# A bound of two on the gathers that GpSimd has unfinished in three graph passes

## The chip, the cores and the metric

The kernel runs on one core of a Trainium2 chip. The metric is the device time of one execution in microseconds (us). The kernel before takes 12057.81 us, the median of three runs (12056.52 to 12058.14).

## The reference

There are 12500 nodes with 48 features and 212500 directed edges, sorted by destination. Four residual layers follow each other, and each starts from relu(layernorm(x)):

```
L0: x = x + segment_sum(h[src] * edge_weight, dst)
L1: gate(edge) * h[dst] * cutoff(edge), summed by src, divided by a sum of multiplicities,
    added to h, layernorm, gamma, beta; x = x + that
L2: a = exp(e - segment_max) / segment_sum(exp); x = x + elu(segment_sum(h[src] * a, dst))
L3: y1 = spmm(h); y2 = spmm(y1); x = x + (h + y1 + y2) / 3
    with spmm(h) = segment_sum(h[src] * edge_weight, dst)
```

Three of these need the same work: gather one row per edge from a table in HBM, multiply it by a scalar of the edge, and sum by destination. These are the weighted sum of L2 and the two spmm of L3. They are the three passes that the change touches.

## The kernel before

Edges are padded to 1664 columns of 128 edges (one edge on each partition). Four columns make a group (G = 4), eight groups make a turn (GB = 8), and there are 416 groups in 52 turns. Nodes stand in blocks of 128. A group's destinations fall into one or more blocks; each pair of a group and a block is a window, and a pass has 512 of them.

The program runs five passes over the edges, one after the other, with short layernorm stages between them. `first_pass` does L0 (1668 gathers, line 504). The second pass does L1 and adds its result into HBM with 1664 scatters (line 1097). `light_pass` (line 720) runs three times, for L2, L3a and L3b, with 1664 gathers each (line 736).

In `light_pass` each engine runs its own loop:

- ScalarE converts the four index columns of a group into the `idx` tile (line 743), and later multiplies each of the group's four gathered tiles in `ring` by the edges' weights (line 756), when the gathers have landed (line 753).
- GpSimd waits for a group's indices (line 733) and issues four indirect DMAs (line 736). Each gathers 128 rows of the table into one slot of `ring`. It waits for nothing else, so its sequencer may hand over gathers as far ahead as indices are staged. `idx` and `ring` have 32 slots (8 groups), and ScalarE stages six groups ahead (LEAD).
- VectorE builds a one-hot matrix of destinations for a window (`hot`, line 789), adds the sum of the window before to `acc` (line 778), and after a group's last window raises `s_done` (line 797). ScalarE stages the next group's indices only after that (line 749).
- TensorE multiplies the one-hot by the weighted rows into PSUM, four fp32 matmuls a window that the profile shows as eight (line 816).

Windows are counted in registers, so VectorE's sequencer runs a dozen register instructions for each (lines 774 to 796). The second pass issues its scatters differently: before each one GpSimd waits on one of K = 4 semaphores until the scatter four places earlier has landed (line 1095) and raises `s_seen` (line 1096). Semaphores are waited on by value and never reset; `order` is 0, 1, 2 for the three light passes.

Of the kernel before, what the change touches and what calls it, by code (L numbers as in the profile page):

```python
# [19 lines left out]
U = G * GB  # L20
NG = -(-E // (P * U)) * GB
T = NG * G
TURNS = NG // GB
# [3 lines left out]
AHEAD = 3  # L27
DEPTH = GB
LEAD = DEPTH - 2
TI = T + LEAD * G  # L30
PARTS = 3
C0 = C + GE
# [17 lines left out]
def gnn_kernel(nc, x, dst_cols, src_cols, dst_rows, src_rows, w_cols, logit_cols, logit_rows,  # L50
# [10 lines left out]
    with ExitStack() as ctx:  # L61
        def sb(name, shape, dt=f32):
            return ctx.enter_context(nc.sbuf_tensor(name, shape, dt))

        def sem(name):
            return ctx.enter_context(nc.semaphore(name))
# [21 lines left out]
        iota = sb("iota", [P, NBW * P], u16)  # L88
        dstf = sb("dstf", [P, TI])
        w = sb("w", [P, TI])  # L90
        cw = sb("cw", [P, T])
        lg = sb("lg", [P, TI])
        adapt = sb("adapt", [P, G + T])
        srow = sb("srow", [P, TI])
        ranges = sb("ranges", [1, NG * 2], i32)
# [12 lines left out]
        idx = sb("idx", [P, DEPTH * G], i32)  # L108
# [165 lines left out]
        with nc.Block() as block:  # L274
# [43 lines left out]
            def _(dve):  # L318
# [3 lines left out]
                for columns in (srow, dstf, w, lg):  # L322
                    nv.memset(columns[:, T:TI], 0.0)
                nv.memset(hid[:, :, :], 1.0)
# [137 lines left out]
        s_seen = sem("s_seen")  # L462
        s_landed_rows = [sem(f"s_landed_rows{j}") for j in range(DEPTH)]
        s_spread = sem("s_spread")
        s_picked = sem("s_picked")
        s_kept = sem("s_kept")
        wn_dve = nc.vector.alloc_register("dve_window")
        wn_act = nc.scalar.alloc_register("act_window")
        wn_pe = nc.tensor.alloc_register("pe_window")
# [250 lines left out]
        def light_pass(order, name, src_table, cols, weights, total, before=None):  # L720
# [7 lines left out]
            with nc.Block() as block:  # L728
                @block.gpsimd
                def _(pool):  # L730
                    with pool.Fori(0, TURNS) as i:
                        for j in range(GB):
                            pool.wait_ge(s_idx, i * GB + (j + 1))
                            pool.sem_inc(s_seen, 1)
                            for u in range(j * G, (j + 1) * G):
                                pool.indirect_dma_start(  # L736
                                    out=ring[:, u, 0:cols], out_offset=None, in_=src_table,
                                    in_offset=bass.IndirectOffsetOnAxis(ap=idx[:, u:u + 1], axis=0)).then_inc(s_landed_rows[j], 16)

                @block.scalar  # L740
                def _(act):
                    def stage(slot, column):
                        nc.scalar.copy(idx[:, slot * G:(slot + 1) * G], srow[:, ds(column, G)]).then_inc(s_idx, 1)  # L743

                    for j in range(LEAD):
                        stage(j, j * G)
                    with act.Fori(0, TURNS) as i:
                        for j in range(GB):
                            act.wait_ge(s_done, i * GB + (j + 1))
                            act.sem_inc(s_seen, 1)  # L750
                            stage((j + LEAD) % DEPTH, i * U + (j + LEAD) * G)

# [543 lines left out]
```

## Time and profile before

| | us |
|---|---|
| median of three runs | 12057.81 |
| span of the profiled execution | 14556.0 |
| GpSimd busy in it | 9189.0 |
| TensorE matmul busy | 6194.2 |
| VectorE busy | 4412.4 |
| ScalarE busy | 3916.7 |

The profiled execution is 2498 us longer than the median of the runs that nobody profiled. The profile gives no time for it beside its span. Its durations are those of one execution with the profiler on.
### The profile page before, as it was taken

Reading aid. Unit: us, or ns where it says so; the run is one execution under the profiler, and the core shown is the slowest. Engines: PE = TensorE matmul, PEld = TensorE weight load, DVE = VectorE, ACT = ScalarE, POOL = GpSimd, SP = SyncE. Lnnn points to the kernel's source line nnn. Section 1 sums busy time; section 2 is a strip of 40 time slices with the busy share of each in tenths; the row PEclk is TensorE's granted clock in tenths of the full one; section 3 lists DMA queues with packets and bytes.
Section 4 is the critical chain, followed back from the end, with each engine's and each line's share of the span. In section 5 each row is a group of like instructions: output and inputs, shape, how many; then the busy total and the mean of one; then the engine's idle time right before and its main releaser. Section 6 shows DMA issues by size and latency. Waiting matters only on the chain. (4 is left out here: it accounts for less than half of the span.)

```text
span 14556.0 us, 229228 instructions
## 1 busy us (share of the span) xinstructions
PE 6194.2 (43%) x41742; PEld 4831.3 (33%) x41743; DVE 4412.4 (30%) x18474; ACT 3916.7 (27%) x13496; POOL 9189.0 (63%) x8348
## 2 busy tenths in 40 slices
PE   4444444444555555552333333333333333333333
PEld 2222222223444444442333333233333333333333
DVE  4444444445444444443111111211111111111111
ACT  3444444443333333321111111111121111111111
POOL 5555555556888888884666666566666656666665
DMA  4333333334455554541111111111111111111111
GB/s 116 100 102 102 99 97 96 96 94 63 61 62 61 61 62 61 62 59 42 16 16 16 16 16 16 20 16 16 16 16 16 16 21 16 16 16 16 16 16 21
DMA packets 805020, 671.18 MB, mean 46 GB/s; under 512 B 417876, under 2 KB 663828, under 8 KB 802727
## 3 DMA queue, kind: packets, MB, share of 16 engines
q0 software_dynamic: 452736, 234.14, 14.8%
q1 hardware_dynamic: 349659, 430.53, 11.2%
q10 hardware_dynamic: 2588, 6.12, 0.1%
q14 instruction: 26, 0.21, 0.0%
q8 instruction: 11, 0.18, 0.0%
HBM read 562.94 MB, written 107.13 MB: 46 GB/s over the span
## 5 line engine op out<-in xcount | busy, mean ns | idle before, releaser
L736 POOL DMA_INDIRECT table<-table,idx x4992 | 4838.7, 969 | 3149.9 <-ACT idx L743 1638.0
L816 PE MATMUL psum_acc<-table 128*128 128x48 f32 (+1 forms) x12288 | 2946.7, 417 | 5074.1 <-DVE acc L778 2363.5
L816 PEld LDWEIGHTS psum_acc<-table 128*128 128x128 f32 x12288 | 2733.0, 328 | 5287.7 <-issue 5244.2
L1097 POOL DMA_INDIRECT sums<-rows,idx x1664 | 2619.5, 1574 | 577.6 <-issue 430.9
L504 POOL DMA_INDIRECT rows<-table,idx x1668 | 1670.2, 1001 | 1581.9 <-ACT idx L556 1059.2
L789 DVE TENSOR_TENSOR table<-iota,dstf 128x512 f32 x1536 | 1064.6, 693 | 3059.2 <-issue 2074.7
L743 ACT CAST idx<-srow 128x4 int32 (+1 forms) x1266 | 243.2, 193 | 6322.7 <-DVEq L797 4262.1
L778 DVE TENSOR_TENSOR acc<-acc,psum_acc x1539 | 311.3, 202 | 3420.0 <-remote 2352.8
L704 PE MATMUL psum_acc<-parts,onehot 128*128 128x48 bf16 x6144 | 338.8, 215 | 1600.5 <-DVE onehot L647 1433.7
L1013 PE MATMUL psum_exp<-table,onet 128*128 x6144 | 432.3, 219 | 1376.2 <-DVE onet L932 1166.2
L756 ACT ACTIVATE table<-table,w 128x48 f32<-128x48 f32 x3328 | 840.6, 323 | 26.2 <-DMA table<-table,idx 12.4
L1013 PEld LDWEIGHTS psum_exp<-table,onet 128*128 128x128 bf16 x6144 | 341.8, 116 | 1510.4 <-issue 1487.5
L704 PEld LDWEIGHTS psum_acc<-parts,onehot 128*128 128x128 bf16 x6144 | 271.8, 117 | 1686.8 <-DVE onehot L647 1500.9
L986 PE MATMUL psum_mlp<-w2s,hid 49*128 49x48 f32 x3336 | 808.3, 414 | 50.8 <-DMA hid<-hid_dram 50.7
L986 PEld LDWEIGHTS psum_mlp<-w2s,hid 49*128 49x128 f32 x3336 | 741.2, 324 | 124.5 <-issue 124.5
L597 ACT ACTIVATE scratch<-drow,far 128x512 f32<-128x512 uint16 x512 | 369.3, 721 | 598.8 <-DVE segmax L666 293.2
L1064 ACT ACTIVATE gate<-psum_mlp,adapt,cw 128x48 f32<-128x48 f32 x1664 | 514.1, 390 | 48.8 <-issue 26.2
L1043 ACT CAST parts<-rest 128x196 bf16<-128x196 f32 x416 | 149.9, 360 | 1281.1 <-DVE rest L913 903.8
L964 DVE TENSOR_TENSOR idx<-srow,dmp 128x4 int32<-128x4 f32 x416 | 67.9, 163 | 1321.3 <-POOLq L1099 1243.8
L691 PE MATMUL psum_mlp<-srcrow,w1s 40*48 40x512 f32 x416 | 396.9, 1056 | 153.3 <-issue 152.2
L573 ACT ACTIVATE prod<-rows,w 128x48 f32<-128x48 f32 x1668 | 426.0, 324 | 54.0 <-issue 39.9
L756 ACT ACTIVATE table<-table,lg 128x49 f32<-128x49 f32 x1664 | 422.0, 325 | 14.2 <-DMA table<-table,idx 9.1
(183 smaller groups left out, 7162.2 us busy)
## 6 DMA issues: line engine op xcount, KB each, us to landing
drow<-rows_dram SPq DMA_DIRECT2D x832, 128.0 KB
lrow<-in_logit_rows SPq DMA_DIRECT2D x416, 256.0 KB
table<-table,idx POOLq DMA_INDIRECT x4992
srcrow<-rows_dram SPq DMA_DIRECT2D x416, 128.0 KB
hid_dram<-hid SPq DMA_DIRECT2D x416, 96.0 KB
hid<-hid_dram SPq DMA_DIRECT2D x416, 96.0 KB
rows<-table,idx POOLq DMA_INDIRECT x1668
sums<-rows,idx POOLq DMA_INDIRECT x1664
```

Of the source, the lines that this page charges most:

```text
L504: pool.indirect_dma_start(out=rows[:, u, 0:width], out_offset=None, in_=src_table, in_offset=bass.IndirectOffsetOnAxis(ap=idx[:, u:u + 1], ...
L573: last = nc.scalar.activation(prod[:, j % 2, u, 0:cols], rows[:, j % RING * G + u, 0:cols], ACT.Copy, scale=weights[:, ds(i * U + (j * G + ...
L691: nc.tensor.matmul(psum_mlp[j % 2][0:C, :], w1s[:, :], attr[j % 2], start=True, stop=True).then_inc(s_mlp1, 1)
L704: last = nc.tensor.matmul(psum_acc[:, 0, 0:cols], onehot[:, u, :], parts[:, j % 2, u, q, 0:cols], start=(u == 0 and q == 0), stop=(u == G ...
L736: pool.indirect_dma_start(out=ring[:, u, 0:cols], out_offset=None, in_=src_table, in_offset=bass.IndirectOffsetOnAxis(ap=idx[:, u:u + 1], ...
L756: last = nc.scalar.activation(ring[:, j * G + u, 0:cols], ring[:, j * G + u, 0:cols], ACT.Copy, scale=weights[:, ds(i * U + (j * G + u), 1)])
L789: nv.tensor_tensor(hot[:, j % 2, :, :], iota[:, ds(k * P, P)].unsqueeze(1).to_broadcast([P, G, P]), dstf[:, ds(i * U + j * G, G)].unsqueez ...
L816: last = nc.tensor.matmul(psum_acc[:, ds(win & 1, 1), 0:cols].rearrange("p r c -> p (r c)"), hot[:, j % 2, u, :], ring[:, j * G + u, 0:col ...
L986: last = nc.tensor.matmul(psum_mlp[j % 2][:, u * C:(u + 1) * C], hid[:, j % 2, u * P:(u + 1) * P], w2s[:, :], start=True, stop=True)
L1013: last = nc.tensor.matmul(psum_exp[j % 2][:, u * CT:(u + 1) * CT], onet[:, u * P:(u + 1) * P], table[:, ds(k, 1), q, :].rearrange("p b c - ...
L1064: last = nc.scalar.activation(gate[:, j % 2, u, 0:C], psum_mlp[j % 2][:, u * C:(u + 1) * C], ACT.Identity, scale=cw[:, ds(t, 1)], bias=ada ...
L1097: pool.indirect_dma_start(out=sums[c], out_offset=bass.IndirectOffsetOnAxis(ap=idx[:, slot:slot + 1], axis=0), in_=rows[:, slot, 0:CS], in ...
```

## The change

Each gather of the three passes gets a second semaphore, `s_begun`, which GpSimd raises by one when the engine has completed the instruction; the first one, `s_landed_rows`, is still raised by 16 when the rows have landed. At the start of the first of the three passes `s_begun` is raised by 2. Before gather number n (counted from 0 over all three passes) GpSimd's sequencer waits for `s_begun` >= n + 1, which holds when gathers 0 to n-2 are complete, and raises `s_seen`.

```diff
+QUEUED = 2
...
+        s_begun = sem("s_begun")
...
                 def _(pool):
+                    if order == 0:
+                        pool.sem_inc(s_begun, QUEUED)
                     with pool.Fori(0, TURNS) as i:
                         for j in range(GB):
                             pool.wait_ge(s_idx, i * GB + (j + 1))
                             pool.sem_inc(s_seen, 1)
                             for u in range(j * G, (j + 1) * G):
+                                pool.wait_ge(s_begun, i * U + (order * TURNS * U + u + 1))
+                                pool.sem_inc(s_seen, 1)
                                 pool.indirect_dma_start(
                                     out=ring[:, u, 0:cols], out_offset=None, in_=src_table,
-                                    in_offset=bass.IndirectOffsetOnAxis(ap=idx[:, u:u + 1], axis=0)).then_inc(s_landed_rows[j], 16)
+                                    in_offset=bass.IndirectOffsetOnAxis(ap=idx[:, u:u + 1], axis=0),
+                                    engine_sem=s_begun).then_inc(s_landed_rows[j], 16)
```

## Rows read from the trace of the kernel before

**Rows 1.** The page's head, and its busy time by engine.

```profile
span 14556.0 us, 229228 instructions
PE 6194.2 (43%) x41742; PEld 4831.3 (33%) x41743; DVE 4412.4 (30%) x18474; ACT 3916.7 (27%) x13496; POOL 9189.0 (63%) x8348
```

**Rows 2.** Groups of POOL instructions: count | busy us, mean ns | idle us before, releasers.

```profile
L736 POOL DMA_INDIRECT table<-table,idx x4992 | 4838.7, 969 | 3149.9 <-ACT idx L743 1638.0 <-issue 1511.9
L1097 POOL DMA_INDIRECT sums<-rows,idx x1664 | 2619.5, 1574 | 577.6 <-issue 430.9 <-ACT rows L1050 76.8 <-DMA sums<-rows,idx 42.6
L504 POOL DMA_INDIRECT rows<-table,idx x1668 | 1670.2, 1001 | 1581.9 <-ACT idx L556 1059.2 <-issue 522.6
```

**Rows 3.** Timeline, one light pass: start us, us, engine, line [idle before <-releaser].

```profile
7999.77 0.95 POOL L736 DMA_INDIRECT table<-table,idx  x1 [0.30 <-issue]
8001.21 0.69 DVE L789 TENSOR_TENSOR table<-iota,dstf 128x512 f32 x1 [1.70 <-issue]
8002.14 1.94 PE L816 MATMUL psum_acc<-table 128*128 128x49 f32 x8 [1.36 <-issue]
8012.26 0.95 POOL L736 DMA_INDIRECT table<-table,idx  x1 [0.30 <-issue]
8013.42 0.21 DVE L778 TENSOR_TENSOR acc<-acc,psum_acc  x1 [11.52 <-remote]
8013.84 0.19 ACT L743 CAST idx<-srow 128x4 int32 x1 [12.91 <-issue]
8014.82 1.02 POOL L736 DMA_INDIRECT table<-table,idx  x1 [1.61 <-issue]
8024.64 1.03 POOL L736 DMA_INDIRECT table<-table,idx  x1 [5.04 <-ACT idx L743]
```

**Rows 4.** First, last and sum of the six stretches without GpSimd's DMAs; the columns ahead.

```profile
core 0: us, PE busy (x) PEld busy (x) DVE busy (x) ACT busy (x) POOL busy (x), PEclk, DMA share, GB/s
0.00:125.00 125.00, 45.24 (x198) 43.11 (x199) 79.32 (x58) 14.44 (x37) 60.67 (x24) 1.00 0.56 148
...
14530.50:14556.00 25.50, 11.49 (x48) 10.69 (x48) 9.98 (x15) 4.87 (x21) 0.14 (x1) 1.00 0.28 96
sum 417.30, PE 95.01 PEld 86.48 DVE 294.00 ACT 83.24 POOL 62.13; mean PE 15.83 PEld 14.41 DVE 49.00 ACT 13.87 POOL 10.36
```

**Rows 5.** Timeline: first gathers of the first and light passes, with later rows of one.

```profile
125.15 1.16 POOL L504 DMA_INDIRECT rows<-table,idx  x1 [32.24 <-ACT idx L556]
...
6645.76 1.02 POOL L736 DMA_INDIRECT table<-table,idx  x1 [103.73 <-ACT idx L743]
...
9321.24 0.94 POOL L736 DMA_INDIRECT table<-table,idx  x1 [69.00 <-ACT idx L743]
...
9324.98 0.95 POOL L736 DMA_INDIRECT table<-table,idx  x1 [0.30 <-issue]
...
9327.62 1.01 ACT L756 ACTIVATE table<-table,w 128x48 f32<-128x48 f32 x4 [1.54 <-DMA table<-table,idx]
...
11919.66 4.91 POOL L736 DMA_INDIRECT table<-table,idx  x1 [23.55 <-ACT idx L743]
```

**Rows 6.** Sequencer instructions by line: count, ns min/median/max (light, second, first, second pass).

```profile
L774 DVEq MOVE  x1536: 3/36/1394, 6652.7 to 14541.7; - x192
L927 DVEq MOVE  x416: 36/36/36, 3407.1 to 6514.6; - x139
L523 SPq MOVE hid_dram<-hid x414: 4/29/717, 150.2 to 3348.9; - x138
L898 SPq MOVE drow<-rows_dram x416: 29/29/29, 3403.4 to 6503.1; - x139
```

**Rows 7.** Second pass: GpSimd's semaphore instruction before each scatter, and two scatters of the timeline.

```profile
L1096 POOLq EVENT_SEMAPHORE  x1660: 17/17/17, 3419.7 to 6536.3; - x185
...
5000.51 1.56 POOL L1097 DMA_INDIRECT sums<-rows,idx  x1 [0.30 <-issue]
...
5011.67 1.56 POOL L1097 DMA_INDIRECT sums<-rows,idx  x1 [0.30 <-issue]
```

## The prediction

> **What bounds the kernel now.** I read the busy time by engine first. GpSimd is the busiest engine at 63% of the span, and nothing else reaches half [rows 1]. The groups of its instructions come next. Three lines hold all its DMAs: 4992 gathers of the light passes, 1664 scatters, 1668 gathers of the first pass, and beside their busy time stand 3149.9, 577.6 and 1581.9 us of idle time [rows 2]. That idle time has two kinds. "issue" is a fixed gap between one DMA and the next. In the timeline the ten steps from 7999.77 to 8012.26 are 1.249 us each, 0.945 busy and 0.304 gap [rows 3]. The other kind is starvation: 1638.0 us in the light passes and 1059.2 us in the first pass, in which GpSimd waits for ScalarE's indices [rows 2].
>
> So the profiled execution is not bound by GpSimd alone. The timeline shows why. TensorE ended a window's matmuls at 8004.08, VectorE's next addition started only at 8013.42, after 11.52 us of idle time, and ScalarE staged the next indices right behind it, at 8013.84 [rows 3]. All that time GpSimd worked off gathers that it had been handed before, and at 8024.64 it stood still for 5.04 us for lack of indices [rows 3]. What VectorE did is in the sequencer rows: its register move in the light passes, usually 36 ns, takes up to 1394 ns, and the same kind of move in the second pass takes 36 ns every time [rows 6]. SyncE's move shows the same, up to 717 ns in the first pass and 29 ns always in the second [rows 6]. The first and the light passes let GpSimd run far ahead. The second holds it to four unlanded scatters. Few unfinished DMAs and no slow sequencers go together.
>
> Now the question is whether this stall is in the runs without the profiler. I build the time that GpSimd alone would need. Busy: 4838.7 + 2619.5 + 1670.2 = 9128.4 [rows 2]. Gaps: 4992 + 1664 + 1668 = 8324 DMAs at 0.304 make 2530.5. The stretches without its DMAs add 417.3 [rows 4]. The sum is 12076.2, and the median is 12057.8, 0.15% less. From the other side: the profiled span is 2498 us above the median, and its starvation is 1638.0 + 1059.2 = 2697, less the four waits between stages. Those are 32.2, 103.7, 69.0 and 23.6 [rows 5]; 2469 is left. The profile's extra time is nearly the starvation, and no more. I take it that the unprofiled kernel is bound by GpSimd at the trace's own pace in all five passes, and that the slow sequencer is the profiler's. A second sign: some slow moves are recorded with 3 or 4 ns, less than a move takes [rows 6], as if it were the writing of the records that was held up.
>
> **The change part by part.** The time is set by 4992 gathers of 0.969 + 0.304 = 1.273 us, 6355 us in all. 0.2% of the median (24 us, about what a measurement of this kernel can tell from no change) is 5 ns a gather.
>
> Added on GpSimd's sequencer, for each gather: a register operation for the waited value, the wait, and a semaphore instruction of 17 ns. The second pass has just this before each of its scatters: 1660 semaphore instructions of 17 ns, with a wait ahead of each, and the scatters still follow each other by 11.16 / 6 = 1.86 us with the same 0.30 gap [rows 7]. The instructions hide under the DMA before. I take 0.
>
> The wait itself: gather n is handed over when n-2 is complete. Behind it in the queue stand only the later gathers and the waits for indices, and ScalarE waits for those gathers' landing. Without the wait, n starts 0.30 + 0.95 + 0.30 = 1.55 us after n-2 ends. From a semaphore to a gather's start I read 0.79 us: ScalarE's cast ends at 8014.03, the gather starts at 8014.82 [rows 3]. That leaves 0.76 us of cover. If the completion is reported later than 0.76 us after the recorded end, the pace becomes (0.95 + delay + 0.79) / 2. I take 0, from the second pass, where the wait is even for landings.
>
> What a completion signal costs in the engine no row shows. From below: nothing, or a gain, if the gather's 25 ns between its usual 944 and its mean of 969 shrink (125 us in all). These are collisions with VectorE, not with the queue, so I exclude most of that. From above: a gather into an idle queue is sometimes 1.02 us instead of 0.94 [rows 3], and 0.08 x 4992 = 399 us. But the gather at 9321.24, after 69 us of idle time, takes 0.94 [rows 5]. I take 0 and keep 399 as the end. A rule that speaks against the change stands in the Trainium skill, GPSIMD Engine Reference, Instruction dispatch: an instruction's completion gates what waits on its semaphore, but doesn't hold back the next Pool instruction. The change makes it hold back the next but one; by that rule the queue gives overlap away, and the price is what the cover above fails to hide.
>
> Removed: the run-ahead. If few queued gathers are what frees VectorE's sequencer, as in the second pass, the profile's starvation in the light passes goes: 1638.0 - 103.7 - 69.0 - 23.6 = 1441.7, less a normal gap at each of 289 waits (88), 1354 us. The issue gaps beyond 0.304 add 1511.9 - 4700 x 0.304 = 83. The profiled span would fall by 1437 to 13119. What is late next is GpSimd itself. In the runs that count none of this is there to remove, by the sum above.
>
> The sum against the profiled execution is therefore 14556 - 1437 = 13119, and against the median 12058 + 0. I round the small chance of leftover starvation into 12055.
>
> **The rivals.** First, the stall is real without the profiler too (faster). Then GpSimd's pace in the runs must be shorter than in the trace, so that pace and starvation add up to the same 12058. If half of the 2464 us of starvation and long gaps is there (the first pass's 1027 and the light passes' 1437), the gap would be 0.304 - 1232 / 8324 = 0.156 us, and the change gives 718 back: 11340. The whole would be 10621. For it: slow moves show wherever GpSimd's queue is deep, and no row can tell the profiler's part in them from the machine's. Against it: the sum of GpSimd's own time and the difference of starvation would both agree with the median by accident.
>
> Second, a small cost per gather (slower): the completion signal lengthens each gather or its gap. It has its place in GpSimd's queue, and it counts from 5 ns up. 20 ns make 100 us, 12158; the end is 12457.
>
> Third, the completion comes with the landing (slower). The fourth gather ends at 9325.93 and ScalarE starts on the group at 9327.62, so landing is at most 1.69 us behind the end [rows 5]. The pace would be (0.95 + 1.69 + 0.79) / 2 = 1.715 us, 0.466 above 1.249, times 4992: 2326 us, 14380. It decides from a delay of 0.76 us. The Trainium skill, Perfetto Trace Analysis, DMA Instruction — SWDGE, says that the recorded end is the last descriptor written, not the end of the transfer, and leaves open which unit triggers further semaphore updates; the 1.69 us between end and use agree with the first half.
>
> Fourth, the change doesn't do what it says: the semaphore is raised when the engine takes the gather, not when it ends. Then the queue still shrinks by what is handed over early, the time is 12058, and the profile keeps its stalls.
>
> **How the numbers follow.** Forecast and fourth rival, no change: 0.42, the latter 0.05 of it. First rival, the stall is real: 0.28. Second, small cost: 0.18. Third, landing: 0.07. The remaining 0.05 is leftovers of a few tens of us, 0.03 faster and 0.02 slower. Faster 0.31, same 0.42, slower 0.27. The range goes down to a quarter of the starvation, 12058 - 359 = 11699, and up to 50 ns a gather, 12058 + 250 = 12308; beyond lie about 0.12 and 0.08. The forecast's own range is 12034 to 12082.
>
> **What would show it.** Right: in the changed kernel's profile gathers still follow each other by 1.249 us with a 0.30 gap, VectorE's moves at L774 stay near 36 ns, ScalarE's indices come early and the span is near 13119, while the median stays. Wrong: a gap above 0.31 or a gather above 0.95 (second rival); gathers in pairs about 1.7 us apart (third); a median that falls with the span (first); slow moves and a span near 14556 (the cause of the stall misread, or the fourth).

## The result, and the profile after

| | before | after |
|---|---|---|
| median of four runs, us | 12057.17 | 12132.91 |
| lowest and highest | 12050.06, 12058.14 | 12122.11, 12136.92 |
| ratio, 95% interval | | 1.0062 [1.0048, 1.0076] |
| span of the profiled execution | 14556.0 | 12132.1 |

The change makes the kernel 75.7 us (0.6%) slower, which by the interval is 58 to 92 us. The forecast was no change, 12055.

One thing has to be said first of the span. The trace on which the prediction rests is of a disturbed execution: a second trace of the same kernel (e0_before, below) has a span of 12049.3 us. So the 2424 us between 14556.0 and 12132.1 are not the change's doing, and from here on the trace of e0_before stands for before.

First, the page's head and GpSimd's groups in the changed kernel. They answer to [rows 1, 2]; the line numbers have moved by 2 to 7.

```profile
span 12132.1 us, 239213 instructions
PE 6209.4 (51%) x41742; PEld 4831.1 (40%) x41743; DVE 4453.5 (37%) x18474; ACT 3815.8 (31%) x13496; POOL 9184.1 (76%) x8348
L742 POOL DMA_INDIRECT table<-table,idx x4992 | 4801.2, 962 | 1773.6 <-DMA table<-table,idx 1502.6
L1104 POOL DMA_INDIRECT sums<-rows,idx x1664 | 2624.3, 1577 | 578.4 <-issue 429.4
L506 POOL DMA_INDIRECT rows<-table,idx x1668 | 1697.6, 1018 | 545.7 <-issue 472.2
```

The same groups in the undisturbed trace of the kernel before:

```profile
span 12049.3 us, 229228 instructions
L736 POOL DMA_INDIRECT table<-table,idx x4992 | 4804.5, 962 | 1700.2 <-issue 1511.6 <-ACT idx L743 188.5
L1097 POOL DMA_INDIRECT sums<-rows,idx x1664 | 2620.6, 1575 | 576.7 <-issue 426.5 <-ACT rows L1050 72.9 <-DMA sums<-rows,idx 52.0
L504 POOL DMA_INDIRECT rows<-table,idx x1668 | 1691.0, 1014 | 545.7 <-issue 466.8 <-ACT idx L556 78.9
```

A gather of the light passes takes 962 ns in both. What grew is the idle time before the gathers, 1700.2 to 1773.6: 73.4 us, nearly the whole loss. GpSimd's waits say in what pieces. The columns are total us, times, longest us; first after, then before:

```profile
POOL table L742 <- DMA table<-table,idx: 1502.6, 4932, 0.3
POOL table L742 <- ACT idx L750: 179.5, 3, 103.9
POOL table L742 <- issue: 91.5, 57, 1.8
```

```profile
POOL table L736 <- issue: 1511.6, 4958, 0.3
POOL table L736 <- ACT idx L743: 188.5, 34, 103.9
```

4932 of the 4992 gaps are the usual 0.30 us. Their label has changed from "issue" to the completion semaphore, and nothing else about them has. Then there are 57 waits of 91.5 us together, up to 1.8 us long. Before, no wait of this kind lasted over 0.3 us. Listed one by one, 54 of them are gaps of 1.42 to 1.76 us, mostly 1.70. In each light pass the first stands before gather 113 (counted from 0), and the others come 88 gathers apart. 54 x (1.70 - 0.30) = 75.6 us; added up one by one, the 54 gaps are 74 us longer than 54 usual ones. One of them in GpSimd's timeline of the changed kernel:

```profile
8081.69 0.94 POOL L742 DMA_INDIRECT table<-table,idx  x1 [0.30 <-DMA table<-table,idx]
8082.94 0.94 POOL L742 DMA_INDIRECT table<-table,idx  x1 [0.31 <-DMA table<-table,idx]
8085.58 0.94 POOL L742 DMA_INDIRECT table<-table,idx  x1 [1.70 <-issue]
8086.83 0.94 POOL L742 DMA_INDIRECT table<-table,idx  x1 [0.30 <-DMA table<-table,idx]
```

The sequencer's records of the same stretch (start us, ns, operation, line) show where the 1.70 us come from:

```
8081.421    17 EVENT_SEMAPHORE  741
8081.958    32 ALU_OP           740
8082.669    17 EVENT_SEMAPHORE  741
8085.366    32 ALU_OP           740
8085.441    17 EVENT_SEMAPHORE  741
```

After the semaphore instruction the sequencer hands the gather over and then goes on to the next register operation. That takes 8081.958 - 8081.421 = 0.54 us as a rule. The handover that began at 8082.669 took 2.70 us, 2.16 more.

Sequencers are fast again: the register move at L774, 3/36/1394 ns in [rows 6], is 36/36/43 in e0_before and the same at L781 in the changed kernel, and SyncE's is 29/29/37.

```profile
L774 DVEq MOVE  x1536: 36/36/43, 5637.0 to 12027.4; - x192
L523 SPq MOVE hid_dram<-hid x414: 29/29/37, 141.7 to 2323.9; - x138
```

```profile
L781 DVEq MOVE  x1536: 36/36/43, 5649.9 to 12110.6; - x192
L525 SPq MOVE hid_dram<-hid x414: 29/29/37, 142.8 to 2331.0; - x138
```

### The profile page after: what moved, and what is told of

Its sections match the earlier page's. It is cut to its first block and busy times, and to the rows that moved or that the text cites. A ratio compares the mean times of both kernels' runs of the same rounds, so it can differ in the third digit from the quotient of the medians.

```text
span 12132.1 us, 239213 instructions
## 1 busy us (share of the span) xinstructions
PE 6209.4 (51%) x41742; PEld 4831.1 (40%) x41743; DVE 4453.5 (37%) x18474; ACT 3815.8 (31%) x13496; POOL 9184.1 (76%) x8348
## 3 DMA queue, kind: packets, MB, share of 16 engines
q0 software_dynamic: 452736, 234.14, 17.8%
## 5 line engine op out<-in xcount | busy, mean ns | idle before, releaser
L742 POOL DMA_INDIRECT table<-table,idx x4992 | 4801.2, 962 | 1773.6 <-DMA table<-table,idx 1502.6
L506 POOL DMA_INDIRECT rows<-table,idx x1668 | 1697.6, 1018 | 545.7 <-issue 472.2
```

What stands on the lines that cost most here:

```text
L506: pool.indirect_dma_start(out=rows[:, u, 0:width], out_offset=None, in_=src_table, in_offset=bass.IndirectOffsetOnAxis(ap=idx[:, u:u + 1], ...
L742: pool.indirect_dma_start(out=ring[:, u, 0:cols], out_offset=None, in_=src_table, in_offset=bass.IndirectOffsetOnAxis(ap=idx[:, u:u + 1], ...
```

## The experiments

Ratios are to runs of the kernel before on the same chip, in the same rounds. Differences in us are the ratio's, at 12060.

**e0_before** is the kernel before, unchanged.

> The kernel before, unchanged, once more, for its trace. The trace of before had a span of 14556 us where every other execution takes 12057. Theory A (the stall and the slow sequencers belong to that one profiled execution): this span is within 10 us of 12057, no register move of VectorE above 100 ns, GpSimd starved under 100 us in the light passes, each light pass some 2100 us. Rival (they are in every execution under the profiler): a span near 14500 again. In either case I look for a gather that GpSimd's sequencer takes 2.70 us to hand over, where it takes 0.54 us for the others: the changed kernel's trace has one every 88 gathers, counted from the 113th of each light pass.

Measured: 12067.49 us, ratio 0.9998 [0.9989, 1.0007], span 12049.3. GpSimd waits for indices for 188.5 us in the light passes, and all but some 10 of that are the three waits between stages (103.9, 58.9 and 16.4). From the first start to the last, the passes' gathers take 2102, 2109 and 2112 us. Theory A holds. The long handover can't be told apart here: the records mark a group's start only, and most groups' handovers take 4.9 us, near the 5.0 us of four gathers, as if the sequencer were held by a full queue. It can be seen in the first trace, where starvation kept the queue short. A group's four handovers take 1.88 us there, and 4.05 us in 54 of the 1248 groups, 22 groups (88 gathers) apart. So the event was in the trace that I predicted from, all 54 times.

Eighteen times it even shows there as a gap. Only the first gather of a group waits for indices, so nothing in the program holds back the other three. Yet 18 of those others have a gap above 0.34 us, 1.32 to 1.68 us long, and all 18 stand at the same places, 113 plus a multiple of 88. One of them, gather 1081 of the first light pass, in the first trace:

```profile
8338.19 0.94 POOL L736 DMA_INDIRECT table<-table,idx  x1 [5.14 <-ACT idx L743]
8340.81 0.94 POOL L736 DMA_INDIRECT table<-table,idx  x1 [1.68 <-issue]
8342.05 0.94 POOL L736 DMA_INDIRECT table<-table,idx  x1 [0.30 <-issue]
```

**e1_q32**: the wait never holds.

```diff
-QUEUED = 2
+QUEUED = 32
```

> All that the change adds stays, the completion semaphore and the wait and the semaphore instruction before each gather, but 32 gathers may be unfinished, so the wait never holds. Theory T1 (the 75 us are 54 long handovers of 2.16 us more than usual, which a queue of two covers for 0.76 us and leaves 1.40 us of each bare: 54 x 1.40 = 76): 12057, no gap of GpSimd near 1.70 us in the light passes. T2 (the completion signal costs each gather 15 ns) and T3 (the added instructions cost each gather 15 ns): 12133.

Measured: ratio 0.9996 [0.9987, 1.0005], -5 us (-16 to +6). No gap above 0.34 us within a light pass. The signal, the wait and the instructions together cost nothing that can be told from 0. T2 and T3 fall. The long handovers are still there: the sequencer's records have 54 of 2.70 to 2.77 us at the same places, and the queue hides each of them whole.

**e4_signal_only**: the completion semaphore without a wait.

```diff
-                                pool.wait_ge(s_begun, i * U + (order * TURNS * U + u + 1))
-                                pool.sem_inc(s_seen, 1)
```

> The completion semaphore alone: each gather raises it and nobody waits on it. T1: 12057. T2 (signal costs 15 ns a gather): 12133. T3 (the instructions cost it): 12057.

Measured: ratio 0.9996 [0.9987, 1.0005]. A gather takes 964 ns on average here and 962 in e0_before, with the same gaps, so T2 falls a second time.

**e2_q3**: three unfinished gathers.

```diff
-QUEUED = 2
+QUEUED = 3
```

> Three unfinished gathers instead of two. T1: one more gather covers 1.249 us more, so 1.40 - 1.25 = 0.15 us of each of the 54 long handovers stays bare: 12057 + 8 = 12065, and the gaps at every 88th gather are 0.45 us instead of 1.70. T2 and T3: 12133, with 1.70 us gaps as before or none.

Measured: ratio 1.0004 [0.9995, 1.0013], +5 us (-6 to +16). The time alone can't tell 8 from 0, but the trace can: where the changed kernel has 1.70 us, this one has 49 longer gaps, mostly of 0.45 and together 7 us longer than usual ones, as expected.

```profile
5892.94 0.94 POOL L742 DMA_INDIRECT table<-table,idx  x1 [0.30 <-DMA table<-table,idx]
5894.19 0.94 POOL L742 DMA_INDIRECT table<-table,idx  x1 [0.30 <-issue]
5895.58 1.42 POOL L742 DMA_INDIRECT table<-table,idx  x1 [0.45 <-DMA table<-table,idx]
```

**e5_q4**: four (`QUEUED = 4`).

> Four unfinished gathers cover 2.50 us more than two: T1: nothing bare, 12068, the time of before, no gap near every 88th gather. Rival (the limit itself costs a little at any depth): 3 to 8 us above before, as with three.

Measured: ratio 1.0002 [0.9993, 1.0011]. The longest of its 4894 waits for the completion is 0.3 us, and no gap within a pass is above 0.34, though the 54 long handovers are in its records too. With four, and with 32 (e1_q32), the limit costs nothing that can be told from 0.

```profile
POOL table L742 <- DMA table<-table,idx: 1492.2, 4894, 0.3
```

**e3_q1**: one (`QUEUED = 1`).

> One unfinished gather. T1's cover is worked out from a chain: completion to semaphore 0.03 us, usual handover 0.54, handover's end to the start 0.21. With one gather nothing of it is hidden: the pace is 0.944 + 0.78 = 1.73 us instead of 1.25, 4992 x 0.48 = 2400 us, and each 88th handover is bare in full, 56 x 2.16 = 121 us: 14590 in all. If the cover of two were something else than this chain (a fixed price of the long handover, whatever the queue), the pace would stay near 1.25 and the time near 12140.

Measured: 14590.43 us, ratio 1.2105 [1.2083, 1.2127]. The gap is 0.79 us where 0.78 was worked out, the pace 1.73 us, and 54 gaps, at the same places, are 2.95 to 3.01 us, mostly 2.95, which is 0.79 + 2.16. So the chain behind the 0.76 us of cover is right in each of its parts, and the long handover costs its full 2.16 us where nothing covers it. It comes by the count of gathers and not by the clock: 88 gathers take some 156 us here and some 112 us in the changed kernel.

```profile
6147.70 0.95 POOL L742 DMA_INDIRECT table<-table,idx  x1 [0.79 <-DMA table<-table,idx]
6149.44 0.95 POOL L742 DMA_INDIRECT table<-table,idx  x1 [0.79 <-DMA table<-table,idx]
6153.39 0.95 POOL L742 DMA_INDIRECT table<-table,idx  x1 [3.01 <-issue]
```

**e6_more_instr**: more sequencer instructions, still with two gathers.

```diff
                                 pool.sem_inc(s_seen, 1)
+                                pool.sem_inc(s_seen, 1)
+                                pool.sem_inc(s_seen, 1)
+                                pool.sem_inc(s_seen, 1)
```

> The changed kernel with three more semaphore instructions (s_seen) ahead of each gather. What makes a handover long? T1a (a count of gathers): still every 88th gather, gaps of 1.70 + 3 x 0.08 = 1.94 us as the instructions take cover away, 54 x 1.64 = 89 us above before. T1b (the sequencer's own instruction stream, 3.4 instructions a gather now and 6.4 then): every 46th or 47th gather, some 100 gaps, 170 us above before.

Measured: ratio 1.0078 [1.0063, 1.0094], +94 us (76 to 113). The gaps stand at the same gathers, 113 and then every 88th, and most are 1.93 us. The event is tied to the gathers and not to the instruction stream (T1a). By the trace the instructions cost only what they take from the cover, 0.23 us, and only at those 54 gathers: the 54 gaps are 13 us longer in all than in the changed kernel. The time excludes T1b's 170 us, but can't tell 94 from the 75.7 of the change, as the intervals overlap.

```profile
5893.46 0.95 POOL L745 DMA_INDIRECT table<-table,idx  x1 [0.31 <-DMA table<-table,idx]
5896.34 0.94 POOL L745 DMA_INDIRECT table<-table,idx  x1 [1.93 <-issue]
```

**e7_half_rows** and **e8_quarter_rows**: smaller gathers.

```diff
-                                    out=ring[:, u, 0:cols], out_offset=None, in_=src_table,
-                                    in_offset=bass.IndirectOffsetOnAxis(ap=idx[:, u:u + 1], axis=0),
+                                    out=ring[0:64, u, 0:cols], out_offset=None, in_=src_table,
+                                    in_offset=bass.IndirectOffsetOnAxis(ap=idx[0:64, u:u + 1], axis=0),
```

> The changed kernel, but each gather of the light passes fetches the rows of the first 64 partitions only; the other 64 edges of a column are left out. T1c (the long handover comes when a ring of descriptors has been gone through, some 9 a gather and DMA engine with the one that raises the semaphore, 5 with half the rows): every 88 x 9/5 = 158th gather. T1a (a count of DMAs): every 88th. The time falls with the gather's own; how far, no row says.

Measured, one run: 11991.6 us. The first long handover of a pass is that of gather 128, and the others come 100 apart: neither 158 nor 88. The long handover itself takes 2.98 us instead of 2.70 (the gap is 2.02 or 2.03 us, as the shorter gather also covers less), and a gather takes 934 ns on average instead of 962. My count of places was wrong in its slope, which called for the next run, with `0:32`.

> The changed kernel with the rows of the first 32 partitions only in each gather of the light passes; the other 96 edges of a column are left out. With 128 rows the first long handover of a pass is that of gather 113 and the next ones come 88 apart, with 64 rows 128 and 100. 113 x 9 = 1017 and 128 x 8 = 1024; 88 x 9 = 792 and 100 x 8 = 800: as if a ring of 1024 places took 9 for a gather of 128 rows and 8 for one of 64. R1 (8 is the least that a gather takes): 128 and 100 again with 32 rows. R2 (the places go on falling with the rows, 7.5 then): about 137 and 106. R3 (a count of gathers that chance moved): 113 and 88.

Measured, one run: 11876.11 us, first at 128 and then every 100 again (R1). A ring of 1024 places, of which a gather of 128 rows takes 9 and one of 64 or 32 rows 8, fits the first places (1017 and 1024). It doesn't give the intervals, which would be 792 and 800 places, and the software DMA queue has the same 452736 packets in the changed kernel and in both of these, so no record shows the 9 and the 8 either. The extra time goes with the interval: 2.16 us / 88 = 24.5 ns and (2.98 - 0.54) / 100 = 24.4 ns. That is as if the sequencer took back the places of 88 or 100 finished gathers one by one. It isn't a price for each gather since the last long handover: the first one of a pass, with 113 gathers before it, takes 2.70 us like the others. No record shows what the sequencer does, so what makes the handover long is open.

```profile
5790.78 0.90 POOL L742 DMA_INDIRECT table<-table,idx  x1 [0.30 <-DMA table<-table,idx]
5793.71 0.90 POOL L742 DMA_INDIRECT table<-table,idx  x1 [2.03 <-issue]
```

```profile
5793.50 0.87 POOL L742 DMA_INDIRECT table<-table,idx  x1 [0.30 <-DMA table<-table,idx]
5796.44 0.86 POOL L742 DMA_INDIRECT table<-table,idx  x1 [2.08 <-issue]
```

No experiment points to a version faster than the kernel before: the limit costs or is free, and it gives nothing back.

## Why the prediction was right or wrong

**The bound: right.** GpSimd sets the time in all passes. The sum of 12076.2 from [rows 2, 4] was made with the busy times of the disturbed trace, and e0_before shows nearly the same ones (4804.5, 2620.6 and 1691.0, which is 9116.1 instead of 9128.4) with hardly any starvation. The light passes have a second proof: in e7_half_rows the gathers are 138 us shorter in all, and the time is 141 us shorter than that of the changed kernel.

**The stall: right in what mattered.** I took the slow sequencers and 2469 us of starvation to be that profiled execution's own. e0_before has neither. "The slow sequencer is the profiler's" was too much said, though: e0_before and nine other traces were taken with the profiler as well and have no such stall. What disturbed that one execution is open. A deep queue alone doesn't do it, as e0_before has one and no slow register move. Whether a short queue would have cured it is open too, as no run met the disturbance again. The 1437 us that the changed profile was to lose, and 13119 for its span, can't be tested against 14556, since their starting point is gone.

**Added instructions and signal, taken at 0: right** (e1_q32, e4_signal_only).

**The wait itself, taken at 0: wrong, and here the forecast failed.** The sentence was "That leaves 0.76 us of cover. If the completion is reported later than 0.76 us after the recorded end [...] I take 0." The 0.76 us are right (e3_q1 confirms the chain behind them), and completions aren't late: in e3_q1 the semaphore rises 0.01 us after the recorded end, and the sequencer goes on 0.02 us later. But I held the cover against one danger only, a late completion. The other side of the chain, the handover, I took from a single example, 0.79 us from semaphore to start [rows 3]. One handover in 88 takes 2.16 us longer. The run-ahead used to hide it whole; a queue of two hides 0.76 of it, and 54 x 1.40 = 75.6 us are left. The first trace had it in view: the 83 us of "issue gaps beyond 0.304", which I counted as part of the stall, hold the 18 gaps shown above (23 us beyond the usual 0.30). The support that I drew from the second pass was weak for the same reason: its scatters may be four deep, and e5_q4 shows for gathers that at four deep the cost is gone.

The rule that I cited from the Trainium skill, GPSIMD Engine Reference, Instruction dispatch, pointed the right way, as the price is what the cover fails to hide. e3_q1 is its extreme: with each instruction held back by the completion before it, the gap is 0.79 us instead of 0.30.

**The rivals.** The first (stall real, faster) falls with e0_before and e1_q32. The second had the right sign and by luck about the right size of time, "20 ns make 100 us", but not the mechanism: a gather takes 962 ns as before, and nothing is paid per gather. Its sign of being wrong, "a gap above 0.31", came true 54 times, for another cause. The third (completion with the landing) falls: the pace is 1.249 us and not 1.715. The fourth falls too: the semaphore rises 0.01 us after the gather's recorded end, and the limit does bind (e3_q1).

**The size.** 0.2% was 24 us, and the loss is 75.7. The wide range of 11699 to 12308 holds it, but was made for other causes; the forecast's own 12034 to 12082 doesn't.

## What to carry to other kernels

A limit on run-ahead is priced by the rarest step that the run-ahead hides, not by the median one. Before counting a queue's cover, list the whole distribution of each link of the chain (here 1248 group handovers, of which 54 took 4.05 us instead of 1.88), look into every gap that no wait of the program explains, and take (longest link - cover) x count. And when a profiled span lies 20% above the runs, take a second trace before building on its stalls.

## What the runs showed of the hardware

- Handing an indirect DMA over holds GpSimd's sequencer for 0.54 us, and the engine starts it 0.22 us later at the earliest (e3_q1). Its completion semaphore rises 0.01 us after its recorded end, and a waiting sequencer goes on 0.02 us after that.
- Every 88th handover (100th for DMAs of 64 or 32 rows) takes longer, by 2.16 us for 88 and 2.44 us for 100, from gather 113 (128) of each light pass on. One unfinished gather leaves 2.16 us of that bare, two 1.40, three 0.15, four nothing.
- A gather's time on GpSimd hardly depends on its rows: 962 ns on average for 128, 934 for 64 and 910 for 32, which is 5% less for a quarter of the rows.
